# Picking message rows with TensorE: 49 one-hot blocks a tile, or seven blocks against seven spans of nodes at once

## What is computed

```python
h = jnp.maximum(_layernorm(x), 0.0)
# layer 0
hw = h @ W0 + b0
agg = segment_sum(w[:, None] * hw[src], dst); deg = segment_sum(w, dst)
x = x + relu(agg / (deg[:, None] + 1e-06))
# layer 1
h = jnp.maximum(_layernorm(x), 0.0)
m = gelu(concat([h[src], edge_attr]) @ W_msg + b_msg)
x = x + gelu(((1 + eps) * h + segment_sum(m, dst)) @ W_upd + b_upd)
```

## Time and profile before

| | |
|---|---|
| device time, median of 3 runs | 3269.75 us (3269.13 to 3270.3) |
| the profiled execution: span of its trace | 3271.2 us |
| TensorE busy / weight loads | 97% / 95% |
| VectorE busy | 82% |
| GpSimd busy | 73% |
| ScalarE busy | 60% |
| one-hot matrices on VectorE (L1100) | 1372 instructions, 2119.6 us |
| gathers (L499) | 1250 and 1274, 1181.0 and 1202.6 us |

### The profile page before, as it was taken

How to read it: one execution, slowest core, us unless ns; L and a number is a source line. 1 busy time by engine, 2 the same in 40 slices (tenths; PEclk the granted TensorE clock), 3 DMA queues, 4 the chain that set the end, 5 groups by cost and what they waited for, 6 DMA issues and landing times.

```text
span 3271.2 us, 104825 instructions
## 1 busy us (share of the span) xinstructions
PE 3160.8 (97%) x39149; PEld 3111.0 (95%) x39150; DVE 2685.9 (82%) x3320; ACT 1949.2 (60%) x6683; POOL 2399.7 (73%) x2539
## 2 busy tenths in 40 slices
PE   3999999999999999999889999999999999999999
PEld 3999999999999999999889999999999999999999
DVE  8888888888888887888688888888888888888885
ACT  5666666666666666666465555555555555555554
POOL 5777777777777777777467777777777777777775
PEclk9999999999999999999899999999999999999999
DMA  6333333333333333333233333344434443333342
GB/s 143 72 79 75 71 82 71 71 74 78 73 74 71 71 71 74 78 73 80 55 85 100 101 100 101 100 101 100 101 100 102 99 104 101 103 101 102 104 103 58
DMA packets 524716, 286.46 MB, mean 88 GB/s; under 512 B 283002, under 2 KB 458618, under 8 KB 524678
## 3 DMA queue, kind: packets, MB, share of 16 engines
q1 hardware_dynamic: 443910, 203.09, 23.2%
q0 software_dynamic: 80768, 82.87, 13.3%
HBM read 280.25 MB, written 5.50 MB: 87 GB/s over the span
## 4 chain that ended last, share of the span: by engine, by line
POOL 64%; issue 23%; PE 9%; DVE 2%; POOLq 1%; DMA 0%; ACT 0%; DVEq 0%; SPq 0%; ACTq 0%
POOL rows L499 64%; PE ps L762 4%; PE ps L769 2%; PE ps L798 1%; DVE pick_all L1100 1%; PE ps L866 1%; PE ps L791 0%; POOLq L495 0%; PE ps L826 0%; PE ps L896 0%; POOLq L510 0%; DMA rows<-h_table,idx 0%; DVE x_sb L1142 0%; POOLq L497 0%; DVEq L1158 0%
## 5 line engine op out<-in xcount | busy, mean ns | idle before, releaser
L1100 DVE TENSOR_SCALAR pick_all<-src_bc,node_f 128x2688 bf16<-128x2688 int16 x1372 | 2119.6, 1604 | 29.8 <-issue 28.9
L762 PE MATMUL ps<-parts,pick_all 128*128 128x192 bf16 x19208 | 1640.2, 246 | 24.7 <-DVE pick_all L1100 22.2
L762 PEld LDWEIGHTS ps<-parts,pick_all 128*128 128x128 bf16 x19208 | 1587.9, 98 | 36.2 <-issue 19.5
L499 POOL DMA_INDIRECT rows<-p_table,idx x1274 | 1202.6, 944 | 402.3 <-issue 402.3
L499 POOL DMA_INDIRECT rows<-h_table,idx x1250 | 1181.0, 945 | 390.8 <-issue 388.3
L769 PE MATMUL ps<-parts,pick_all 128*128 128x192 bf16 x9604 | 856.4, 246 | 5.5 <-issue 4.8
L769 PEld LDWEIGHTS ps<-parts,pick_all 128*128 128x128 bf16 x9604 | 797.2, 98 | 9.5 <-issue 8.4
L591 ACT ACTIVATE onehot<-iota,dw 128x72 f32<-128x72 f32 x1568 | 405.9, 342 | 0.0
L591 ACT ACTIVATE h_sb<-iota,dw 128x72 f32<-128x72 f32 x1568 | 405.9, 343 | 0.0
L1297 DVE TENSOR_TENSOR room<-ps,rows 128x512 f32<-128x512 f32 x196 | 135.5, 692 | 243.5 <-DMA rows<-p_table,idx 243.4
L523 ACT CAST idx<-src_tab 128x8 int32 (+1 forms) x392 | 78.1, 200 | 420.6 <-DMA rows<-h_table,idx 420.5
(11 more groups left out here) (108 smaller groups left out, 1706.3 us busy)
## 6 DMA issues: line engine op xcount, KB each, us to landing
src_bc<-last_src SPq DMA_DIRECT2D x196, 448.0 KB
ea<-in_edge_attr_dram SPq DMA_DIRECT2D x196, 256.0 KB
src_bc<-last_src SPq DMA_DIRECT2D x196, 224.0 KB
rows<-p_table,idx POOLq DMA_INDIRECT x1274
rows<-h_table,idx POOLq DMA_INDIRECT x1250
h_sb<-last_src SPq DMA_DIRECT2D x24, 224.0 KB
x_sb<-in_x_dram SPq DMA_DIRECT2D x12, 224.0 KB, 3.9
h_table<-h_sb SPq DMA_DIRECT2D x6, 224.0 KB
```

The source lines that it names most:

```text
L499: nc.gpsimd.indirect_dma_start(out=rows[:, s, j, 0:D], out_offset=None, in_=table[:, :], in_offset=bass.IndirectOffsetOnAxis(ap=idx[:, s, ...
L762: last = nc.tensor.matmul(psG[(s + shift) % 2], pick[layer][(s + shift) // 2 % 2][:, n, at:at + P], parts[:, n, :], start=(n == 0), stop=( ...
L1100: last = nc.vector.tensor_scalar(pick[layer][i][:, c * KB:(c + 1) * KB, :], src_bc[:, i, :, 0:w], node_f[:, c:c + 1], None, ALU.is_equal)
```

## The change

A node number is split into `a * 896 + k * 128 + p`: seven spans `a`, seven blocks `k` in a span. VectorE compares with the number modulo 896, so the one-hot matrix of a tile has only seven blocks (`KA`), and each block of it multiplies the rows of all seven spans at once: 7 x 64 = 448 columns. The three parts are summed in PSUM by running the same seven blocks against each part: 21 matmuls of 448 columns a tile. What comes out for an edge is seven candidate rows, and VectorE multiplies them with a mask that has a one at the edge's span and sums over the spans.

The number of picked tiles becomes 2, 2, 1, 2 in the four slots of layer 0 (343 in all, 1225 gathered) and 2, 1, 2, 1 in layer 1 (294 and 1274). The extra halves, the `y` tile and the reload of `x` go. All loops run over single bodies.

```diff
-    parts = sb("parts", [P, NB, SPLIT * D], bf16)
+    parts = sb("parts", [P, SPLIT, KA, NA, D], bf16)
+    mask = sb("mask", [P, NG, NPM, NA], bf16)
+    NP = ((2, 2, 1, 2), (2, 1, 2, 1))
+    JP = [[J - n for n in NP[layer]] for layer in range(2)]
+    BANKS = ((1, 4), (3, 5))
...
-                for n in range(NB):
-                    last = nc.tensor.matmul(psG[(s + shift) % 2], pick[layer][(s + shift) // 2 % 2][:, n, at:at + P],
-                                            parts[:, n, :], start=(n == 0), stop=(n == NB - 1))
+                pe.wait_ge(s_pick[layer], g + 1)
+                if q:
+                    pe.wait_ge(s_prow[layer], g)
+                else:
+                    pe.wait_ge(s_parts[layer], UNITS)
+                for t in range(n):
+                    to = ps[:, BANKS[layer][q % 2] + t, 0:NA * D]
+                    for k in range(KA):
+                        for part in range(SPLIT):
+                            last = nc.tensor.matmul(to, hot[:, k, t * P:(t + 1) * P],
+                                                    parts[:, part, k, :, :].rearrange("p a d -> p (a d)"),
...
-            def pick_half(layer, i, half):
+            def make_pick(layer, b, q):
+                n, _ = picks_of(layer, q)
+                dve.wait_ge(s_bc[layer][q % 2], (b * (SLOTS // 2) + (q // 2 + 1)) * 16)
+                nc.vector.tensor_scalar(pick_all[:, q % 2, 0:KA * n * P].rearrange("p (k e) -> p k e", k=KA),
+                                        src_bc[:, q % 2, :, 0:n * P], node_f[:, 0:1], None,
+                                        ALU.is_equal).then_inc(s_pick[layer], 1)
...
+            def picked_rows(layer, b, q):
+                dve.wait_ge(s_picked[layer], g + 1)
+                dve.wait_ge(s_used[q % SLOTS], b + (layer * BODIES + q // SLOTS + 1))
+                nc.vector.tensor_tensor(sel[:, 0:n, :, :],
+                                        ps[:, bank:bank + n, 0:NA * D].rearrange("p t (a d) -> p t a d", d=D),
+                                        of.unsqueeze(3).to_broadcast([P, n, NA, D]), ALU.mult).then_inc(s_sel, 1)
+                nc.vector.tensor_reduce(rows[:, q % SLOTS, J - n:J, 0:D],
+                                        sel[:, 0:n, :, :].rearrange("p t a d -> p t d a"),
                                         AX.X, ALU.add).then_inc(s_prow[layer], 1)
...
-            with nc.Fori(0, TWOS, engines=(mybir.EngineType.PE,), hint_back_edge=True) as c:
-                for odd in range(2):
-                    first(c, odd, False)
+            with nc.Fori(0, BODIES - 1, engines=(mybir.EngineType.PE,), hint_back_edge=True) as b:
+                first(b, False)
```

More of the change, by code:

```diff
@@ L296, in two_layer_gnn, with picks_of @@
         block = ctx.enter_context(nc.Block())
[L298 to L303, removed]
+        def picks_of(layer, q):
+            n = NP[layer][q % SLOTS]
+            return n, NPM - n
         def unit(t, u):
@@ L318, in _ @@
         def _(sp):
[L321 removed]
+            for one in (*s_used, *s_prow):
                 sp.sem_inc(one, 1)
@@ L766, in extra @@
-            def extra(layer, i, half):
-                for n in range(half * NB // 2, (half + 1) * NB // 2):
-                    last = nc.tensor.matmul(psX, pick[layer][i][:, n, PE2:PE3], parts[:, n, :],
-                                            start=(n == 0), stop=(n == NB - 1))
-                return last
-            def next_gathers(layer, b, s):
-                i = (s + 1) // 2 % 2
-                if s % 2:
-                    gather(layer, b, s, 1)
-                    if EXTRA[layer][i]:
-                        pe.wait_ge(s_xrow[layer], extras(layer, b + (s + 1) // SLOTS, i) - 1)
-                        extra(layer, i, 0)
-                else:
-                    if EXTRA[layer][i]:
-                        extra(layer, i, 1).then_inc(s_xpicked[layer], 1)
-                    gather(layer, b, s, 1)
@@ L786, in gather_y, with picks @@
-            def gather_y(c):
-                pe.wait_ge(s_ypick, c + 1)
-                pe.wait_ge(s_yrow, c + 1)
-                for n in range(NB):
-                    last = nc.tensor.matmul(psY, pick_y[:, n, :], parts[:, n, :], start=(n == 0), stop=(n == NB - 1))
-                last.then_inc(s_ypicked, 1)
+            def picks(layer, b, q):
+                g = b * SLOTS + q
+                n, _ = picks_of(layer, q)
+                hot = pick_all[:, q % 2, 0:KA * n * P].rearrange("p (k e) -> p k e", k=KA)
+                pe.wait_ge(s_pick[layer], g + 1)
+                if q:
+                    pe.wait_ge(s_prow[layer], g)
+                else:
[6 more added lines that the diff above has]
+                                                    parts[:, part, k, :, :].rearrange("p a d -> p (a d)"),
+                                                    start=(k == 0 and part == 0),
+                                                    stop=(k == KA - 1 and part == SPLIT - 1))
+                last.then_inc(s_picked[layer], 1)
```

365 lines of the change are left out of this document (135 added, 230 removed).

## The result

| | before | after |
|---|---|---|
| device time, median | 3269.44 us (3268.53 to 3270.3) | 3348.89 us (3348.1 to 3349.1) |
| span of the profiled execution | 3271.2 us | 3346.9 us |
| last gather of layer 0 starts | 1596.57 | 1649.81 |
| first product of the stretch between | 1605.79 | 1674.99 |
| first gather of layer 1 | 1656.52 | 1719.26 |

The ratio is 1.0243, with a 95% interval of 1.0229 to 1.0258. The sign was forecast; 3349 lies far outside the range of 3272 to 3308. The span grew by 75.7 us: 69.2 until the first product of the stretch (26.5 were forecast), then 6.5 back until the first gather of layer 1 (6.0 were forecast), nothing in layer 1's gathers, and 13.0 in the tail after the last gather, where nothing was forecast. The timed medians differ by 79.4 us, 59 more than the forecast's 20.5, and the spans by 75.7, 55 more.

What follows compares the result with a forecast made beforehand. GpSimd's gathers were taken to bound both layers before, TensorE layer 0 after. Layer 0 ending 26.5 us later, less 6.0 given back between the layers, made 20.5 us more: 3290 us, range 3272 to 3308.

Steps and rivals of the forecast that it cites:

- the sum for layer 0: Start, 343 picked tiles, 194 windows, pass ends and closing path: next stretch begins at 1632.3 instead of 1605.79, 26.5 us later.
- The matmul of 448 columns: TensorE's picks: 186.7 ns for the columns plus 2.5 fixed, 189.2 ns each, a tile 3.97 us.
- The first pick: Start of layer 0: one matrix and the modulo steps suffice, so TensorE's first pick starts at about 54.1, not 60.59.
- The stretch gave 6.5 us back (6.0): Between the layers: TensorE idles less, its clock stays full, and shorter products and waits save 6.0 us.
- the gathers don't speed up: Against rival 5, that gathers quicken when VectorE falls silent: 1% would be 25 us, chance 0.02.
- the 119 of the prediction: Reading between the skill page's real-stream figures: some 119 ns for 448 columns, a tile of 2.5 us.
- The reduction, 448 elements at 0.62, 1.1 for 896: VectorE's sum over spans in slot 1's masking path: 1.1 us of a path of 4.7 us.
- I put no stall: Layer 0, slot 1: the masking path of 4.7 us fits under 4.97 us of TensorE work, so no wait counted.
- Rival 3: Layer 0's mask path too long from strided reads or a broadcast operand: 39 us more, 3329; chance 0.16, small stalls included.
- 0.3 us of room: Layer 0, slot 1: what the 4.7 us masking path leaves of the 4.97 us before window 1 needs it.
- 48 x 0.28 = 13.4 us: TensorE's loss at loop pass ends in layer 0: 48 passes at 0.28 us, 13.4 us; 0 if hidden, 17 at most.
- below GpSimd's 32.47: nothing on the path: Layer 1: TensorE's body falls from 32.38 to about 32.0 us, under the gathers' 32.47, so no effect on time.

Runs made afterwards that it cites:

- b_sel: Changed kernel with the masked product written so that the reduction reads its seven candidates side by side; 3315.2 us, ratio 1.0129.
- c_busy: Changed kernel with 72 idle matmuls instead of 28 ahead of the last windows of layer 1; 3338.55 us, ratio 1.0197.
- f2_675: Changed kernel with b_sel's order of sums, four bodies a pass, 6.75 tiles a body in layer 0, 72 idle matmuls in the tail; 3270.8 us, ratio 1.0001.
- h2_675b: f2_675 with 84 idle matmuls instead of 28 ahead of the last window of layer 0 as well; 3278.72 us, ratio 1.0022.
- e2_pass4: b_sel with four bodies of layer 0 in one loop pass, seven tiles in every body; 3304.2 us, ratio 1.0101.

## Why the prediction was wrong in size and right in sign

**Right.** A body of seven tiles makes TensorE the bound of layer 0. With the reduction repaired the sum for layer 0 holds: b_sel's first product of the stretch comes at 1635.86, forecast were 1632.3, and the 3.6 us left are the pass ends of point 2 below. The matmul of 448 columns is 189.1 ns (189.2 was taken), so columns set the price. The first pick starts at 53.88 (54.1). The stretch gave 6.5 us back (6.0), its mean granted clock 0.89 from 1674 to 1720. Layer 1's gathers are 1.2487 us apart from 1719.26 to 3308.84, as in the earlier trace rows, with VectorE at 47% instead of 82% busy: the gathers don't speed up.

On the price of a matmul the Trainium skill is not borne out: "TensorE: Matmul & The Clock Gate", section "Back-to-back issue gap", has 131 ns for 512 columns in a real stream. The stream here has a weight load for each matmul and runs at 189.1 ns for 448, which is the page's formula for the isolated stream. A straight line between the page's two figures gives 123 ns for 448 columns, not the 119 of the prediction, and a tile of 2.6 us; the measurement refutes either.

**Wrong, and by how much.**

1. "The reduction, 448 elements at 0.62, 1.1 for 896": 1.70. This was the step that failed. The row I scaled it from, L999 in the earlier trace rows, reads elements that lie together; L1043 reads one in every 256 bytes. The rest of the chain's excess, some 0.2 us, is the later start of the product and small gaps. With it "I put no stall" fell: 0.49 us of wait a body, and 0.31 behind it. 48 x 0.80 = 38 us. Rival 3 had this mechanism, "strided reads", and its 3329 would have been nearer. That its 39 us meet the 38 is luck: it slowed the product too, which took 1.09 us as planned, and it had no 0.31 us behind the wait. It was given 0.16, although 0.3 us of room is less than the error that a chain of five estimates can have. With b_sel's edit the chain fits, but with 0.1 us of room and not 0.3. The Trainium skill's "SBUF — State Buffer", in section "Door 1: The DMA port swizzle (why `[64,N]` ≈ `[32,N]`)", has a rule that bears on this: accesses that leave a line of 16 bytes each time pay for it. The runs agree for that memory: 1.70 against 1.09 us for 896 elements.
2. "48 x 0.28 = 13.4 us" for the pass ends: 0.35 each, 16.8 us, 3.4 us more. Right in kind, and inside the range given.
3. Together with 0.02 us in the picks and windows, the body is 32.96 instead of 32.07 us, and 48 x 0.89 = 42.7 us is the whole shortfall at the first product of the stretch (1674.99 - 1632.3); smaller misses at the start and the end of the layer cancel.
4. The tail, 13.0 us, was in no term. "below GpSimd's 32.47: nothing on the path" was true of the gathers and wrong of what follows the last one. A TensorE that runs ahead in layer 1 stands idle for 4.82 us ahead of its last windows, where it was 0.45 before. I had seen the same effect at the end of layer 0, with the sign turned, and did not ask it of the second end. c_busy shows the 13 us.

42.7 + 13.0 - 0.5 (more given back in the stretch) = 55.2 of the 55.2 us between the forecast span change of 20.5 and the measured 75.7.

## What to carry to other kernels

When two engines share a job, the time is that of the worse of the two, and a share of 7 or 6 in a body is coarse: mix bodies, and let the lighter one be the last. Then look again for what each engine loses at the end of a longer pass: here VectorE's 3.7 us came out from under the cover and cost TensorE 2 us a pass. Time a chain that must fit under another piece of work from instructions with the same strides as well as the same size; if the room is less than what a factor on one term would take, put the stall in the sum. When an engine gains slack in a loop, look at its idle time at the loop's last turn: there the clock may fall just before serial work (13 us here).

## What the runs showed of the hardware that I had not expected

- A reduction on VectorE of float32 in steps of 256 bytes takes 1.70 us for 896 elements and 0.92 for 448; with elements that lie together 1.09 and 0.62. A product that reads PSUM in steps of 256 bytes takes the same 1.09 us as one that reads it in order.
- The end of a pass costs TensorE 0.35 us after one body of 211 matmuls and as many weight loads, and 0.50 + 0.36 us after four. VectorE is idle there for 0.54 us after one body and for 3.7 after four.
- A window that waits 0.49 us for ScalarE delays the picks behind it by 0.31 us more, in every body; without the wait there is no such gap. The cause is open.
- An idle time of 4.82 us before serial work cost the tail 13 us; with two waits of 0.94 and 0.91 us the profiled tail was 37.2 us in f2_675, with 0.98 and 0.91 it was 25.3 in h2_675b, which has the same layer 1. What decides between them is open.
- On the chip where the kernel before took 5500.15 us, the four kernels with merged picks took 4972.0 to 5093.25 us, ratios of 0.905 to 0.925. TensorE's weight loads waited there for nothing that the profile names, 8.4 us in e2_pass4 on the other chip and 612.3 here, with the same code and the same stretch, from 100 to 1600 us:

```profile
PEld ps L720 <- issue: 612.3, 1067, 2.7
```

The new way of picking was 7.5 to 9.5% faster there. That this comes from its fewer and longer instructions is a guess, since the kernel before was not profiled on that chip; and what disturbed the chip is not known.
